# The rotation's sum of the later tiles on GpSimd, and the clamp as a paired maximum on VectorE

## The chip, the core and the metric

The kernel runs on one core of a Trainium2 chip. A core has TensorE (matrix products into PSUM), VectorE, ScalarE (activations), GpSimd and SyncE (which issues transfers), each with its own queue of instructions in the order in which the program gives them; they meet only by semaphores. All read and write SBUF; TensorE writes PSUM. The metric is the device time of one execution in microseconds (us). In the profile TensorE is PE, VectorE DVE, ScalarE ACT, GpSimd POOL.

## What is computed

Four stages on 4 x 512 tokens of 128 numbers, each `x = x + f(layernorm(x))`: a linear recurrence, a stack of two attention and feed-forward layers with a window of 64 tokens, one full attention, and a mixture of 32 experts. The change lies in the second stage, where each layer does this to its queries and keys:

```python
def l2norm(t):
    return t / jnp.clip(jnp.linalg.norm(t, axis=-1, keepdims=True), 1e-12)
...
h = shift_token(x)
qkv = h @ wqkv
q, k, v = jnp.split(qkv, 3, axis=-1)
...
q = l2norm(q) * qs
k = l2norm(k) * ksc
...
q = q * cos * scale + rotate_half(q) * sin * scale
k = k * cos / scale + rotate_half(k) * sin / scale
```

Then come scores in windows, softmax, the product with the values, and the feed-forward part with a GELU gate.

## The kernel before

**Tiling.** The second stage is cut into blocks of 512 tokens (4 batches x 2 layers = 8 blocks) and these into 4 tiles of 128 tokens, tile n of 32. A tile's queries and keys are 128 rows x 1,024 numbers (8 heads of 64, twice).

**One tile n, by the engine that does it.**
- TensorE: the product for queries and keys (L1527, L1528), then for values (L1533).
- ScalarE: the squares (L811). VectorE: `squares_sum(n)`, sums of squares over 64 (L1085), then the clamp at 1e-24 (L1088).
- GpSimd: `inverse_lengths(n)`, the power -1/2 of the 16 clamped sums (L682), called the power here.
- VectorE: `normalise(n)` (L1093), PSUM to SBUF.
- VectorE: `scale_cos(n)`, times cosine (L1102), into `rot`. GpSimd: `rotate(n)`, the two halves times sine, swapped (L690, two instructions), into `rotb`. For tiles 0 and 1 VectorE does these too.
- VectorE: its own `rotate(n)`, `rot = rot + rotb` (L1110), called the sum.
- TensorE: `heads_T(n)`, transposes of `rot` (L1542), and the scores (L1569). VectorE: maximum and subtraction (L1115, L1118). TensorE: transposes of the probabilities (L1579). ScalarE: exponentials (L837). TensorE: times the values (L1594), transposes (L1602), the output product (L1613). VectorE: `o_out(n)`, divides by the sum (L1125, L1128).

**Order.** `layer_steps()` writes out one order of steps, and every engine's program walks through it and does its own part of each item. Step i of the tile loop does, among others: transposed probabilities of tile i, squares of tile i + 3 (`ssq`), output of tile i, `heads` of tile i + 1, the sum of tile i + 2 (`rotsum`), normalise of tile i + 3 (`norm`), feed-forward `up` with its GELU and gate (L862, L1145), scores of tile i + 1, output transposes of tile i, product for queries and keys of tile i + 4, and last `rot` of tile i + 3, where L1102 and L690 stand. Steps with i mod 4 = 3 also have the transposes of the next block (L1513, L1080) and `base`, the bias added to a block's stream on GpSimd (L698, in the second layer L702 too). Steps with i mod 4 = 0 add a block's attention output and copy half of it (L1135, L1139); i mod 4 = 1 have the statistics of the feed-forward layernorm; i mod 4 = 2 a block's result (L1650, L1154).

**The end of the loop.** Steps 28 to 31 are written out by hand, with pieces of the third stage between them. At step 27's end VectorE applies the layernorm of the third stage's batch 0 (L1037, four instructions). `split` of batch 0 follows `rot` of tile 31: GpSimd forms rests of numbers cut to bf16 (L734, L737, two each), SyncE stores them and loads them again in another layout, and TensorE's `max` takes them (L1761).

Of the kernel before, what the change touches and what calls it, by code (L numbers as in the profile page):

```python
# [10 lines left out]
ALU = mybir.AluOpType  # L11
ACT = mybir.ActivationFunctionType
AX = mybir.AxisListType

P = 128
BATCH, SEQ = 4, 512
TOK = BATCH * SEQ
NT = SEQ // P
# [5 lines left out]
LAYERS, HEADS, DH, WIN = 2, 8, 64, 64  # L24
# [28 lines left out]
EW = 2 * INTER + IC * P  # L53
SKIP = 1e30
ROUNDER = 2.0 ** 23
AHEAD, WBUF = 4, 5
ROWS_AHEAD = 8

# [13 lines left out]
def build(nc, A, out):  # L72
    with ExitStack() as ctx:
        def sb(name, shape, dt=FP):
            return ctx.enter_context(nc.sbuf_tensor(name, shape, dt))

        def sem(name):
            return ctx.enter_context(nc.semaphore(name))
# [22 lines left out]
        sq = part(region_a, 2 * INNER)  # L101
# [21 lines left out]
        rot = [part(region_r, 2 * INNER) for _ in range(2)]  # L123
        rotb = [part(region_r, 2 * INNER) for _ in range(2)]
# [22 lines left out]
        stats = [sb(f"stats{i}", [P, NT, 6]) for i in range(2)]  # L147
        mv = [sb(f"mv{i}", [P, NT, 2]) for i in range(2)]
        rstd = [sb(f"rstd{i}", [P, NT]) for i in range(2)]
        ssum = sb("ssum", [P, 2 * HEADS])  # L150
        ssum_c = [sb(f"ssum_c{i}", [P, 2 * HEADS]) for i in range(2)]
        nbias = [sb(f"nbias{i}", [P, NT]) for i in range(2)]
        zero4 = sb("zero4", [P, NT])
# [96 lines left out]
        def bank(n, width=BANK, of=1):  # L250
# [3 lines left out]
        S = {n: sem(n) for n in (  # L254
            "a_in", "tab_in", "par_in", "wqkv_in", "w_in", "warm", "ones_f", "tabs", "idn", "zero_p",
            "ln_stats", "ln_mv", "ln_eps", "ln_rstd", "ln_out", "ln_neg", "ln_act", "xnT_mm", "scanned", "bc_mm", "x1",
            "yT_mm", "hT_lo", "hT_hi", "qk_mm", "v_mm", "squared", "ssq", "ssq_c", "rnormed", "normed", "rot_a",
            "rot_bb", "rotated", "v_sb", "qkT_mm", "qT_sb", "kT_sb", "s_mm", "smax", "diffed", "pT_mm", "exped", "o_mm",
            "o_rec", "o_norm", "oT_mm", "oT_sb", "wo_mm", "y_att", "hs_lo", "hs_mm", "hs_hi", "based_y", "based",
            "hnT_mm", "hnT_sb", "up_mm", "gelued", "acted", "down_mm", "y_out", "stored")}  # L260
# [180 lines left out]
        for what, n in layer_steps():  # L441
            if what == "l1":
                what, n, i = n
# [38 lines left out]
        def need(engine, semaphore, count):  # L482

            if count > 0:
                engine.wait_ge(semaphore, count)
# [148 lines left out]
        def _(pool):  # L634
            g = nc.gpsimd
# [48 lines left out]
            def rotate(n):  # L684

                pool.wait_ge(S["normed"], n + 1)
                need(pool, S["rotated"], n - 1)
                for half in range(2):
                    dst, src, tab = turned(n, half)
                    g.tensor_tensor(dst, src, tab, ALU.mult).then_inc(S["rot_bb"], 1)  # L690

            def base(k):
                l, s = divmod(k, BATCH)
# [324 lines left out]
        def _(v):  # L1018
            d = nc.vector
# [13 lines left out]
            def norm_apply(m, src, dst):  # L1033
# [5 lines left out]
                                           ALU.subtract, ALU.mult)  # L1039
                last.then_inc(S["ln_out"], 1)  # L1040

            d.memset(ones_f[:, :], 1.0).then_inc(S["ones_f"], 1)
            for p in range(2):
                d.memset(hT[p][64:P, 0:1], 0.0)
# [37 lines left out]
            def squares_sum(n):  # L1082
                v.wait_ge(S["squared"], n + 1)
                need(v, S["ssq_c"], n)
                d.tensor_reduce(ssum[:, :], sq.rearrange("p (h d) -> p h d", d=DH), AX.X, ALU.add).then_inc(S["ssq"], 1)  # L1085
                v.wait_ge(S["ssq"], n + 1)
                need(v, S["rnormed"], n - 1)
                d.tensor_scalar(ssum_c[n % 2][:, :], ssum[:, :], 1e-24, None, ALU.max).then_inc(S["ssq_c"], 1)  # L1088

            def normalise(n):  # L1090
                v.wait_ge(S["rnormed"], n + 1)
# [109 lines left out]
            def whole(dst):  # L1201

                link(d.tensor_scalar(dst, dst, ROUNDER, None, ALU.add))
                link(d.tensor_scalar(dst, dst, -ROUNDER, None, ALU.add))

# [171 lines left out]
            for what, n in layer_steps():  # L1377
# [28 lines left out]
                            d.tensor_tensor(dst, src, tab, ALU.mult).then_inc(S["rot_bb"], 1)  # L1406
                if what == "ssq":
                    squares_sum(n)
                if what == "rotsum":
                    rotate(n)  # L1410
                if what == "scores":
                    scores_out(n)
# [621 lines left out]
```

## Time and profile before

| | |
|---|---|
| median of 3 runs | 656.52 us (655.28 to 659.74) |
| the profiled execution, its own time | 653.41 us |
| its span in the profile | 651.5 us |
| PE busy | 589.5 us (90%) |
| DVE busy | 518.1 us (80%) |
| ACT busy | 363.9 us (56%) |
| POOL busy | 302.8 us (46%) |
| granted PE clock over the span | 0.987 of full |

A row of the timeline has the start, the length, the engine, the line, the operation, output and inputs with their shapes, and the number of instructions merged; in brackets the engine's idle time ahead of it and what ended it. All times count from the span's start. The chain of waits is followed back from the last instruction: at each point to what released it, or to the instruction before it on its engine.

### The profile page before, as it was taken

To read this page: it belongs to the slowest core of one execution; us is meant where nothing else is said; L and a number is where in the kernel's file an instruction comes from. 1 tells how busy PE (TensorE), PEld (TensorE's weight loads), DVE (VectorE), ACT (ScalarE), POOL (GpSimd) and SP (SyncE) were. 2 spreads that over 40 slices of the span, in tenths; PEclk is the share of its full clock that TensorE was granted. 3 is DMA by queue.
4 is the path that set the end of the run, shared out by engine and by line. 5 is a ranking of instruction groups with operands and counts; after the bars stand their busy time and mean duration, and the time that the engine had idled before them with its cause. 6 is when DMAs were issued, how large, how long until landed. Compare 5 with 4: busy or idle time off the path is not lost.

```text
span 651.5 us, 14777 instructions
## 1 busy us (share of the span) xinstructions
PE 589.5 (90%) x5571; PEld 361.4 (55%) x5571; DVE 518.1 (80%) x919; ACT 363.9 (56%) x582; POOL 302.8 (46%) x254
## 2 busy tenths in 40 slices
PE   8787987999999999999999888898899989999994
PEld 7465655766766666667667666554223324454442
DVE  5887888988799798898888975868877776577883
ACT  0243453477566575674775673422675667744882
POOL 4464464555554545555663860524020002162886
PEclk8998999999999999999999999999999999999998
DMA  8313010010110101010010126061976336216431
GB/s 264 99 26 115 18 34 10 18 34 10 24 28 17 28 17 27 17 25 20 17 26 18 35 79 132 2 146 30 225 197 188 99 98 193 95 41 131 63 47 11
DMA packets 33298, 44.04 MB, mean 68 GB/s; under 512 B 9248, under 2 KB 24652, under 8 KB 32460
## 3 DMA queue, kind: packets, MB, share of 16 engines
q1 hardware_dynamic: 26172, 40.97, 23.9%
q0 software_dynamic: 3968, 2.12, 2.4%
q8 instruction: 45, 0.74, 0.5%
q10 hardware_dynamic: 3088, 0.01, 0.3%
q14 instruction: 25, 0.20, 0.1%
HBM read 27.54 MB, written 8.41 MB: 55 GB/s over the span
## 4 chain that ended last, share of the span: by engine, by line
PE 62%; DVE 15%; ACT 6%; issue 6%; POOL 6%; DMA 2%; DVEq 0%; POOLq 0%; SPq 0%; ACTq 0%
PE ps L1594 4%; PE ps L1641 4%; PE ps L1672 4%; PE ps L1542 4%; PE ps L1579 4%; PE ps L1533 3%; PE ps L1879 3%; PE ps L1527 3%; PE ps L1650 3%; PE ps L1613 3%; PE ps L1777 3%; PE ps L1528 3%; PE ps L1569 3%; PE ps L1761 3%; ACT region_r L918 2%
## 5 line engine op out<-in xcount | busy, mean ns | idle before, releaser
L682 POOL TENSOR_TENSOR rnorm<-ssum_c,neg_half 128x16 f32<-128x16 f32 x32 | 94.7, 2960 | 101.4 <-DVE ssum_c L1088 100.0
L690 POOL TENSOR_TENSOR region_r<-region_b,region_w 128x512 f32<-128x512 f32 x60 | 77.8, 1318 | 43.3 <-DVE region_b L1093 42.8
L1317 DVE TENSOR_REDUCE mneg<-ps 128x2 f32<-128x1024 f32 x64 | 77.5, 1221 | 19.8 <-PE ps L1761 18.8
L918 ACT ACTIVATE region_r<-ps 128x1024 f32<-128x1024 f32 x64 | 63.3, 1024 | 32.3 <-PE ps L1777 32.0
L811 ACT ACTIVATE region_w<-ps 128x1024 f32<-128x1024 f32 x32 | 32.8, 1026 | 54.1 <-PE ps L1528 51.3
L1641 PE MATMUL ps<-region_w 128*114 128x512 f32 x96 | 46.0, 604 | 6.2 <-ACT region_w L828 6.1
L647 POOL TENSOR_TENSOR var_eps<-mv,eps 128x4 f32<-128x4 f32 x20 | 4.4, 221 | 95.2 <-DVE mv L1030 95.2
L787 ACT ACT_TABLE_LOAD x37 | 47.5, 1283 | 1.4 <-PEq L2026 0.7
L774 POOL DMA_INDIRECT out<-region_r x24 | 38.3, 1595 | 18.4 <-DVE region_r L1444 11.2
L1594 PEld LDWEIGHTS ps<-region_b,pts 128*64 128x64 f32 x512 | 32.2, 138 | 24.5 <-issue 24.5
L1093 DVE TENSOR_TENSOR region_b<-ps,rnorm 128x1024 f32<-128x1024 f32 x32 | 39.1, 1223 | 8.0 <-POOL rnorm L682 6.9
L837 ACT ACTIVATE pts<-ps 128x512 f32<-128x512 f32 x64 | 34.7, 595 | 18.4 <-PE ps L1579 18.4
L1115 DVE TENSOR_REDUCE smx<-ps 128x8 f32<-128x1024 f32 x32 | 38.9, 1217 | 6.2 <-PE ps L1569 6.2
L1110 DVE TENSOR_TENSOR region_r<-region_r 128x1024 f32<-128x1024 f32 x32 | 43.2, 1351 | 0.3
L1613 PEld LDWEIGHTS ps<-region_w,oT 128*128 128x128 f32 x256 | 33.6, 192 | 15.0 <-issue 12.2
L1102 DVE TENSOR_TENSOR region_r<-region_b,region_w 128x1024 f32<-128x1024 f32 x32 | 40.9, 1278 | 0.0
L1118 DVE TENSOR_TENSOR region_b<-ps,smx 128x1024 f32<-128x1024 f32 x32 | 39.2, 1225 | 1.1
L1527 PE MATMUL ps<-region_w,hT 128*128 128x512 f32 x64 | 33.9, 612 | 6.7 <-DVE region_b L1093 5.5
L1085 DVE TENSOR_REDUCE ssum<-region_w 128x16 f32<-128x1024 f32 x32 | 38.7, 1209 | 1.2 <-ACT region_w L811 1.2
L1569 PE MATMUL ps<-region_w 64*64 64x128 f32 x1024 | 34.9, 276 | 4.9 <-ACT region_w L830 4.9
L843 ACT ACTIVATE oT<-ps 128x512 f32<-128x512 f32 x32 | 18.8, 588 | 36.5 <-PE ps L1602 36.5
L1594 PE MATMUL ps<-region_b,pts 128*64 128x65 f32 x512 | 36.6, 225 | 1.7 <-ACT pts L837 1.7
(291 smaller groups left out, 1466.7 us busy)
## 6 DMA issues: line engine op xcount, KB each, us to landing
region_w<-in_wx SPq DMA_DIRECT2D x16, 768.0 KB, 4.7
region_b<-region_w SPq DMA_DIRECT2D x56, 130.0 KB, 2.3
parts_dram<-region_b SPq DMA_DIRECT2D x6, 384.0 KB, 2.6
xs_dram<-region_w SPq DMA_DIRECT2D x1, 1548.0 KB, 7.4
region_w<-in_wqkv SPq DMA_DIRECT2D x2, 768.0 KB, 9.0
pts<-xs_dram SPq DMA_DIRECT2D x24, 64.0 KB, 2.0
region_w<-parts_dram SPq DMA_DIRECT2D x3, 384.0 KB, 6.8
region_b<-parts_dram SPq DMA_DIRECT2D x3, 384.0 KB, 7.3
```

What stands on the lines that cost most here:

```text
L682: g.tensor_tensor(rnorm[:, :], ssum_c[n % 2][:, :], neg_half[:, :], ALU.pow).then_inc(S["rnormed"], 1)
L690: g.tensor_tensor(dst, src, tab, ALU.mult).then_inc(S["rot_bb"], 1)
L787: act_(warm[:, :], ones_f[:, 0:1], function).then_inc(S["warm"], 1)
L918: act_(dst, bank(l1_bank[what, b, i], of=2), ACT.Exp).then_inc(T["ex"], 1)
L1102: d.tensor_tensor(rot[n % 2].rearrange("p (z h d) -> p z h d", z=2, h=HEADS), qn[n % 2].rearrange("p (z h d) -> p z h d", z=2, h=HEADS), t ...
L1110: d.tensor_tensor(rot[n % 2], rot[n % 2], rotb[n % 2], ALU.add).then_inc(S["rotated"], 1)
L1317: d.tensor_reduce(mneg[b % 2][:, 2 * i:2 * i + 2], bank(l1_bank[what, b, i], of=2) .rearrange("p (q t) -> p q t", q=2), AX.X, ALU.max, neg ...
L1527: mm(bank(n0), lhs, wqkv[l][:, 0:INNER], start=True, stop=True)
L1569: last = mm(bank(4 + par)[w * WIN:(w + 1) * WIN, hp * P:(hp + 1) * P], qT[p][rows, hp, q0:q0 + WIN], kT[p][rows, hp, q0:q0 + P], start=Fal ...
L1594: last = mm(ps[w * WIN:(w + 1) * WIN, c0:c0 + VW], pts[n % 2][:, j, w * WIN:(w + 1) * WIN], vals[:, t, h, :], start=True, stop=True)
L1613: last = mm(bank(3)[:, t * P:(t + 1) * P], oT[n % 2][:, c, :], wo[k // BATCH][:, c, :], start=(c == 0), stop=(c == 3))
L1641: last = mm(ps[0:HW, n0 * BANK:(n0 + 1) * BANK], w1[k // BATCH][:, g, c, :], hnT, start=True, stop=True)
```

## The change

`rot = rot + rotb` of tiles 10 to 31 is done by GpSimd, right behind its two multiplications of the same tile; for tiles 0 to 9 VectorE keeps it in its old place. The constant of the clamp is written once into every second element of `ssum`, the sums of squares are written into the others, and the clamp becomes a reduction with maximum over the pairs.

```diff
+POOL_SUMS = 2 * NT + 2
...
-        ssum = sb("ssum", [P, 2 * HEADS])
+        ssum = sb("ssum", [P, 2 * HEADS, 2])
...
                 for half in range(2):
                     dst, src, tab = turned(n, half)
                     g.tensor_tensor(dst, src, tab, ALU.mult).then_inc(S["rot_bb"], 1)
+                if n >= POOL_SUMS:
+                    pool.wait_ge(S["rotated"], n)
+                    pool.wait_ge(S["rot_a"], n + 1)
+                    pool.wait_ge(S["rot_bb"], 2 * n + 2)
+                    g.tensor_tensor(rot[n % 2], rot[n % 2], rotb[n % 2], ALU.add).then_inc(S["rotated"], 1)
...
+            d.memset(ssum[:, :, 1], 1e-24)
...
-                d.tensor_reduce(ssum[:, :], sq.rearrange("p (h d) -> p h d", d=DH), AX.X, ALU.add).then_inc(S["ssq"], 1)
+                d.tensor_reduce(ssum[:, :, 0], sq.rearrange("p (h d) -> p h d", d=DH), AX.X, ALU.add).then_inc(S["ssq"], 1)
                 v.wait_ge(S["ssq"], n + 1)
                 need(v, S["rnormed"], n - 1)
-                d.tensor_scalar(ssum_c[n % 2][:, :], ssum[:, :], 1e-24, None, ALU.max).then_inc(S["ssq_c"], 1)
+                d.tensor_reduce(ssum_c[n % 2][:, :], ssum[:, :, :], AX.X, ALU.max).then_inc(S["ssq_c"], 1)
...
-                if what == "rotsum":
+                if what == "rotsum" and n < POOL_SUMS:
                     rotate(n)
```

The order of instructions is shown at two places. VectorE, end of step 18 and step 19 before the change, from the cosine product of tile 21 on (names are those of buffers; `ps` is PSUM, `region_r` holds `rot` and `rotb`, `region_b` the normalised tile):

```order
L1102 TENSOR_TENSOR region_r<-region_b,region_w 128x1024
L1085 TENSOR_REDUCE ssum<-region_w 128x16
L1088 TENSOR_SCALAR ssum_c<-ssum 128x16
L1125 RECIPROCAL orec<-ps 128x8
L1128 TENSOR_TENSOR region_r<-ps,orec 128x512
L1080 COPY hT<-ps 64x511
L1110 TENSOR_TENSOR region_r<-region_r 128x1024
L1093 TENSOR_TENSOR region_b<-ps,rnorm 128x1024
L1145 SCALAR_TENSOR_TENSOR region_b<-ps,b,region_w 114x512
```

The same place after it (the lines of the changed kernel are numbered some 7 higher):

```order
L1109 TENSOR_TENSOR region_r<-region_b,region_w 128x1024
L1092 TENSOR_REDUCE ssum<-region_w 128x16
L1095 TENSOR_REDUCE ssum_c<-ssum 128x16
L1132 RECIPROCAL orec<-ps 128x8
L1135 TENSOR_TENSOR region_r<-ps,orec 128x512
L1087 COPY hT<-ps 64x511
L1100 TENSOR_TENSOR region_b<-ps,rnorm 128x1024
L1152 SCALAR_TENSOR_TENSOR region_b<-ps,b,region_w 114x512
```

The sum is gone from between output and normalise, and the clamp is a reduction. GpSimd, from `base` of step 27 to the split of the third stage, before:

```order
L698 TENSOR_TENSOR region_r<-y,b 128x512
L702 TENSOR_TENSOR region_r<-region_r,xr 128x512
L690 TENSOR_TENSOR region_r<-region_b,region_w 128x16x32 x2
L682 TENSOR_TENSOR rnorm<-ssum_c,neg_half 128x16
L690 TENSOR_TENSOR region_r<-region_b,region_w 128x16x32 x2
L734 TENSOR_TENSOR rot_b<-rot_b,region_r 128x512 x2
L737 TENSOR_TENSOR region_r<-rot_b,region_r 128x512 x2
```

And after:

```order
L704 TENSOR_TENSOR region_r<-y,b 128x512
L708 TENSOR_TENSOR region_r<-region_r,xr 128x512
L691 TENSOR_TENSOR region_r<-region_b,region_w 128x16x32 x2
L696 TENSOR_TENSOR region_r<-region_r 128x1024
L683 TENSOR_TENSOR rnorm<-ssum_c,neg_half 128x16
L691 TENSOR_TENSOR region_r<-region_b,region_w 128x16x32 x2
L696 TENSOR_TENSOR region_r<-region_r 128x1024
L740 TENSOR_TENSOR rot_b<-rot_b,region_r 128x512 x2
L743 TENSOR_TENSOR region_r<-rot_b,region_r 128x512 x2
```

Sums of tiles 30 and 31 (L696) now stand ahead of the power of tile 31 and ahead of the split.

## Rows read from the trace of the kernel before

**Rows 1.** Page, part 4: the chain that ended last, shares of the span by engine.

```profile
PE 62%; DVE 15%; ACT 6%; issue 6%; POOL 6%; DMA 2%; DVEq 0%; POOLq 0%; SPq 0%; ACTq 0%
```

**Rows 2.** Chain in order of time (start us, us, engine and line), steps 11, 19, 23.

```profile
179.09 2.04 DVE region_r L1110
...
270.28 2.04 DVE region_r L1110
...
272.35 0.73 DVE region_b L1093
...
276.68 1.09 PE ps L1579 x8
...
315.87 2.03 DVE region_r L1110
```

**Rows 3.** Timeline, GpSimd, steps 18 and 19 (start us, us, engine, line, operation, idle before).

```profile
256.31 2.90 POOL L682 TENSOR_TENSOR rnorm<-ssum_c,neg_half 128x16 f32<-128x16 f32 x1 [5.19 <-DVE ssum_c L1088]
...
267.10 2.90 POOL L682 TENSOR_TENSOR rnorm<-ssum_c,neg_half 128x16 f32<-128x16 f32 x1 [4.06 <-DVE ssum_c L1088]
269.97 1.27 POOL L698 TENSOR_TENSOR region_r<-region_r,b 128x512 f32<-128x512 f32 x1
```

**Rows 4.** Timeline, VectorE, step 18 and the start of step 19.

```profile
256.98 1.22 DVE L1110 TENSOR_TENSOR region_r<-region_r 128x1024 f32<-128x1024 f32 x1
259.24 1.22 DVE L1093 TENSOR_TENSOR region_b<-ps,rnorm 128x1024 f32<-128x1024 f32 x1 [1.04 <-POOL rnorm L682]
...
263.33 1.23 DVE L1118 TENSOR_TENSOR region_b<-ps,smx 128x1024 f32<-128x1024 f32 x1
264.47 1.22 DVE L1102 TENSOR_TENSOR region_r<-region_b,region_w 128x1024 f32<-128x1024 f32 x1
...
266.85 0.17 DVE L1088 TENSOR_SCALAR ssum_c<-ssum 128x16 f32<-128x16 f32 x1
```

**Rows 5.** Timeline, TensorE, steps 18 and 19: L1602, L1579, L1602.

```profile
261.92 0.66 PE L1602 MATMUL ps<-ident,region_r 128*128 128x128 f32 x4
...
265.02 1.04 PE L1579 MATMUL ps<-ident,region_b 128*128 128x128 f32 x8
...
272.89 0.66 PE L1602 MATMUL ps<-ident,region_r 128*128 128x128 f32 x4
```

**Rows 6.** Timeline, GpSimd, end of the loop (steps 27 to 29) and block 1's split.

```profile
365.66 3.48 POOL L690 TENSOR_TENSOR region_r<-region_b,region_w 128x512 f32<-128x512 f32 x2
371.41 2.91 POOL L682 TENSOR_TENSOR rnorm<-ssum_c,neg_half 128x16 f32<-128x16 f32 x1 [2.27 <-DVE ssum_c L1088]
...
378.17 3.20 POOL L734 TENSOR_TENSOR rot_b<-rot_b,region_r 128x512 f32<-128x512 f32 x2
381.34 3.25 POOL L737 TENSOR_TENSOR region_r<-rot_b,region_r 128x512 bf16<-128x512 f32 x2
...
420.79 2.31 POOL L734 TENSOR_TENSOR pts<-pts,region_b 128x512 f32<-128x512 f32 x2 [4.31 <-ACT region_b L899]
```

**Rows 7.** Timeline, VectorE, end of the loop.

```profile
366.75 1.27 DVE L1102 TENSOR_TENSOR region_r<-region_b,region_w 128x1024 f32<-128x1024 f32 x1
367.94 2.06 DVE L1037 TENSOR_SCALAR y<-xr,mv,rstd 128x128 f32<-128x128 f32 x4
...
377.89 1.35 DVE L1102 TENSOR_TENSOR region_r<-region_b,region_w 128x1024 f32<-128x1024 f32 x1
```

**Rows 8.** Timeline, TensorE, the first scores of the next layer.

```profile
399.73 0.59 PE L1761 MATMUL ps<-region_w 96*128 96x512 bf16 x2 [0.47 <-DMA region_w<-parts_dram]
```

**Rows 9.** Timeline ahead of step 0: tile 2's products on GpSimd, then VectorE beside them.

```profile
42.00 4.39 POOL L690 TENSOR_TENSOR region_r<-region_b,region_w 128x512 f32<-128x512 f32 x2 [2.07 <-DVE region_b L1093]
...
41.84 1.22 DVE L1110 TENSOR_TENSOR region_r<-region_r 128x1024 f32<-128x1024 f32 x1
42.97 2.29 DVE L1102 TENSOR_TENSOR region_r<-region_b,region_w 128x1024 f32<-128x1024 f32 x1
45.18 1.21 DVE L1085 TENSOR_REDUCE ssum<-region_w 128x16 f32<-128x1024 f32 x1
```

## The prediction, made before the changed kernel was run

> **What bounds the kernel now.** I read the chain of waits first, by engine. It stands on TensorE for 62% of the span and on VectorE for 15% [rows 1], so VectorE work is worth time only where it is on that 15%.
>
> The chain in order of time shows where that is. A step is one pass of the tile loop. In the step that ends a block's four tiles, the chain leaves TensorE and runs through the rotation's sum (L1110), normalise, gated product, maximum and subtraction on VectorE before TensorE goes on with L1579, the first work of the next step [rows 2]. The sum takes 2.03 to 2.04 us there, and 1.22 elsewhere [rows 4]; so it is in four steps, 11, 15, 19 and 23, of which rows 2 show the first and the last. The reason is beside it: GpSimd's L698 starts at 269.97 for 1.27 us [rows 3], and the sum issued at 270.28 ends at 272.32, about 1.1 us after L698. The two engines do not read side by side. In the other three steps of four the chain stays on TensorE: the subtraction started at 263.33 ends at 264.56, and TensorE takes it up at 265.02 [rows 4, 5], 0.46 us to spare.
>
> **What the change removes.** The sums of tiles 10 to 31 leave VectorE: 22 instructions. Where TensorE leads nothing is gained. In step 19 normalise of tile 22 no longer stands behind the sum (start 272.35, rows 2) but behind the power alone. How much TensorE can use of that: from L1602 to L1579 it takes 265.02 - 261.92 = 3.10 us unhindered, and 276.68 - 272.89 = 3.79 out of step 19 [rows 2, 5]. So the gain is at most 0.69 us a step, 4 × 0.69 = 2.8 us. It is reached if the subtraction ends 0.7 us earlier. Normalise will start 1.2 us earlier (next part); the gated product then waits for its GELU, but the maximum can still start about 1.0 us earlier, so TensorE is the limit and I take all 2.8.
>
> **What it adds on GpSimd, in a usual step.** The trace has no 128x1024 add on GpSimd. The nearest rows: an add of 128x512 takes 1.27 us, so 2.5 for the double [rows 3]; the plain 128x512 pieces at 420.79 take 2.31 for two [rows 6], the lower bound; the upper is the 4.39 us of two products where VectorE holds the reads twice [rows 9]. I take 2.5, since what follows L1102 on VectorE, a reduction and small work, has one input in SBUF. Sum(21) waits for L1102, which ends at 264.47 + 1.22 = 265.69; with 0.08 us for the signal it runs 265.77 to 268.27. Power(22), queued behind it, starts now at 267.10 when the clamp is done [rows 3, 4]; it will start at 268.25: 1.15 us late. Who waits is normalise. In step 18 it starts when the power ends (259.24, after 1.04 us idle, rows 4), so it comes at 260.4 and ends at 261.6; a small output add follows, and the maximum slips 0.1 us, within the 0.46 to spare. That leaves the sum some 0.35 us: the cost is 0 while it stays under about 2.85 us, and I take 0. In steps 20 and 21 VectorE idles about 1 us before the gated product, for its GELU, and that takes the delay. In step 19 the power ends at 271.15 and normalise starts there, 1.2 us earlier than now, as used above. TensorE transposes tile n a whole step later, so that the sum itself comes later costs nothing.
>
> A page of the Trainium skill prices it a little lower: GPSIMD Engine Reference, § 3.1, has an add of 2,048 columns at 4,497 ns, so an estimate of 2.25 us for 1,024. No run here shows it; the loss below would shrink by some 0.5 us.
>
> **The clamp.** A reduction over pairs replaces the 0.17 us scalar maximum [rows 4]: 16 more numbers read. A reduction of 1,024 columns takes 1.21 us [rows 9], so some 0.02 us more, 0.6 us over 32 tiles, in the idle time named; were it 0.2 more each, it would still be inside 0.35. It runs while the new sum reads. The reduction at 45.18 ran its 1.21 us beside a product that ended at 46.39 [rows 9], so I let it pass undelayed. A scalar form would wait: L1037's four took 2.06 us, started behind GpSimd's products [rows 6, 7]. The one memset, before any input has landed, costs nothing.
>
> **What it adds at the end of the loop.** Here GpSimd leads. The products of tile 30 end at 369.14; power(31) starts at 371.41; the split of the next layer (L734, L737) begins at 378.17 behind the products of tile 31 and ends at 384.59; its store and load end in TensorE's L1761 at 399.73, after only 0.47 us of idle [rows 6, 8]. So all delay of this chain above 0.47 us arrives. Two sums enter it.
> - Power(30) is 1.15 late as before, so L702 ends at 366.8. VectorE's L1102 (issued 366.75, rows 7) reads next, then a product, one L1037, a product, one L1037, sum(30), two L1037. That alternation is what rows 9 show: at 43.0 GpSimd's waiting product went between two back-to-back VectorE instructions, and the second of these (2.29 us) went before the next product. Then L1037 ends at about 373.85 and not 370.00, and power(31), behind L1085 and the clamp, starts at 375.3: 3.9 late. If VectorE keeps its turn for all four L1037, sum(30) runs 371.5 to 374.0, and power(31) is 2.6 late.
> - Sum(31) waits for L1102 of tile 31, now 377.89 to 379.24 [rows 7], which is pushed with normalise(31) to end at 383.1 (or 381.8). The sum ends at 385.6 (384.3), and the split's four pieces, with L1110 of tile 31 gone from VectorE, take 4 × 1.15 = 4.6 and not 6.4 us [rows 6]. They end at 390.2 (388.9), 5.6 (4.3) later than 384.59.
> - TensorE itself is some 2 to 4 us late by then, so not all of this is idle time; 0.1 is lost in what cover is left. Loss 5.5, or 4.2.
>
> **Sum.** -2.8 + 5.5 = +2.7 us, or -2.8 + 4.2 = +1.4. I take +2.5, near the first, since rows 9 show the alternation. The profiled execution took 653.41 us (span 651.5), so it would become 655.9; the runs shown have the median 656.52, so 659.0.
>
> **Rivals.**
> - *The end loses nothing (faster, small).* Were the store and load to absorb the delay, only the gain is left: 656.5 - 2.8 = 653.7. For it: the landing of a transfer varies with what else is queued. Against: 0.47 us of idle before L1761 is all the cover there is.
> - *The power becomes late for TensorE in every step (slower).* If the sum takes 3.5 us, it is 0.65 above what the cover allows, in some 14 steps that gain nothing: 9 us; the gain falls by 1 and the end costs 2 more: 656.5 + 2.5 + 12 = 671. It decides from 2.85 us on. For it: the 4.39 us at 42.00. Against: nothing with two SBUF inputs stands behind L1102 on VectorE except at step 27.
> - *The power holds the reads.* At the end of the loop the copy L1139 will fall into power(31). Did it wait for the power's end, normalise(31) would come behind copy, reciprocal and a 512-column product, about 1.1 us: 659.0 + 1.1 = 660.1. Against: the sum issued at 256.98 took 1.22 us while the power ran from 256.31 to 259.21 [rows 3, 4], so I add nothing. The Trainium skill (SBUF — State Buffer, § Who interferes with whom) says that whoever issues first gets the shared pair "for the whole instruction"; on the power the trace disagrees.
> - *More gain than TensorE's room.* If the shorter VectorE queue drew in other waits, 0.3 us in each of 22 tiles, it would be 659.0 - 6.6 = 652.4. Against: those waits are not on the chain.
>
> **Numbers.** Forecast (+1.4 to +2.7) 0.60; end loses nothing 0.18; power holds the reads 0.06; power late in every step 0.07; more gain 0.09. One per cent, 6.5 us, is what a measurement of this kernel can tell from no change. The slow rival (0.07) lies outside it, and so may 0.05 on the fast side: the tail of the last kind, or the gain alone with a low draw of runs, which themselves span 655.3 to 659.7. So faster 0.05, same 0.88, slower 0.07. The range takes in the gain alone and the held reads, with that spread: 653.0 to 662.5. The likeliest case's own range is 656 to 661.
>
> **What would show it.** In the changed profile: sums of 2.5 us on GpSimd; TensorE's L1579 behind steps 11, 15, 19 and 23 not waiting for VectorE, so a four-tile period of 44.9 us, not the 45.6 from 270.28 to 315.87; the other steps as long as now; power starts 1.1 us late; the L1037 group at step 27 stretched to 4 to 6 us; the split ending 4 to 6 us later against the end of step 26, and TensorE idle before the first L1761 for 1.5 to 3 us. It is wrong if the sum is longer than 2.85 us, if the load lands no later, or if TensorE's steps shorten elsewhere.

## The result, and the profile after

| | before | after |
|---|---|---|
| median, measured side by side | 659.34 us (9 runs, 655.28 to 661.79) | 665.47 us (9 runs, 662.36 to 666.32) |
| ratio | | 1.011, interval 1.0085 to 1.0138 |
| span of the profiled execution | 651.5 us | 663.7 us |
| VectorE busy | 518.1 us | 496.4 us |
| GpSimd busy | 302.8 us | 351.3 us |
| granted clock over the span | 0.987 | 0.975 |

The change makes the kernel 6 us slower, outside the range of the prediction (653.0 to 662.5). The kernel after, put on the chip a second time beside others, gave 664.62 us against 657.08 for before, a ratio of 1.014 (1.0105 to 1.0175).

The rows of cost first, from the groups of the page of the kernel after (busy us and mean ns, then the idle time ahead and what ended it). The lines moved by seven or so: the sum on GpSimd is L696, the power L683, normalise L1100, the cosine product L1109, the clamp L1095.

```profile
L683 POOL TENSOR_TENSOR rnorm<-ssum_c,neg_half 128x16 f32<-128x16 f32 x32 | 95.2, 2976 | 21.1 <-DVE ssum_c L1095 19.7
...
L696 POOL TENSOR_TENSOR region_r<-region_r 128x1024 f32<-128x1024 f32 x22 | 52.1, 2367 | 44.4 <-DVE region_r L1109 44.3
L1100 DVE TENSOR_TENSOR region_b<-ps,rnorm 128x1024 f32<-128x1024 f32 x32 | 39.2, 1224 | 44.2 <-POOL rnorm L683 44.0
```

A sum takes 2.37 us on GpSimd, against 1.22 us on VectorE where nothing is in its way [rows 4]. VectorE now idles 44 us for the power.

**The steady part of the loop came out as forecast.** The same place as [rows 3 to 5], steps 18 and 19, in the timeline of the kernel after: GpSimd, then VectorE, then TensorE.

```profile
267.24 2.36 POOL L696 TENSOR_TENSOR region_r<-region_r 128x1024 f32<-128x1024 f32 x1 [1.73 <-DVE region_r L1109]
269.55 2.91 POOL L683 TENSOR_TENSOR rnorm<-ssum_c,neg_half 128x16 f32<-128x16 f32 x1
...
267.03 1.21 DVE L1092 TENSOR_REDUCE ssum<-region_w 128x16 f32<-128x1024 f32 x1
268.27 0.18 DVE L1095 TENSOR_REDUCE ssum_c<-ssum 128x16 f32<-128x32 f32 x1
...
272.50 1.23 DVE L1100 TENSOR_TENSOR region_b<-ps,rnorm 128x1024 f32<-128x1024 f32 x1 [0.82 <-POOL rnorm L683]
...
274.32 0.66 PE L1609 MATMUL ps<-ident,region_r 128*128 128x128 f32 x4
...
277.42 1.04 PE L1586 MATMUL ps<-ident,region_b 128*128 128x128 f32 x8
```

The power starts 1.1 us behind the end of the clamp (269.55 against 268.45), the reduction and the clamp run beside the sum at their usual 1.21 and 0.18 us, and in step 19 TensorE's L1586 follows the product ahead of it with no wait: 277.42 - 274.32 = 3.10 us where it took 3.79 before [rows 5]. From the scores of tile 8 to those of tile 27 the trace has 213.91 us after and 216.79 before: 2.88 us gained, forecast 2.8.

**The end of the loop lost 8.5 us, not 5.5.** By chance both traces have the scores of tile 28 at 363.10 us. The first scores of the third stage (L1761 before, L1768 after) start at 399.73 before [rows 8] and at 408.19 after. The change of the loop thus makes -2.9 + 8.5 = 5.6 us, where the two measurements have 6.1 and 7.5. The spans of the two traces differ by 12.2 us, since 2.9 us more lie ahead of the scores of tile 8 after, and 3.7 us more behind the first scores of the third stage. None of the moved sums stands there, and the paired clamp, which does stand in the first part, isn't the cause: the kernel only_30, below, has it too and reaches the scores of tile 8 at 133.74 us, before does at 135.34.

TensorE after, in the timeline from the scores of tile 28 on:

```profile
363.10 1.04 PE L1576 MATMUL ps<-region_w 64*64 64x128 f32 x32
...
375.00 1.22 PE L1631 MATMUL ps<-region_r,down_one 128*128 128x256 f32 x2 [3.81 <-DVE region_r L1142]
...
378.80 1.92 PE L1576 MATMUL ps<-region_w 64*64 64x128 f32 x32
...
390.91 1.42 PE L1576 MATMUL ps<-region_w 64*64 64x128 f32 x32 [2.77 <-ACT region_w L836]
...
393.17 4.50 PE L1648 MATMUL ps<-region_w 128*114 128x512 f32 x8
...
408.19 0.60 PE L1768 MATMUL ps<-region_w 96*128 96x512 bf16 x2
```

The same place before:

```profile
371.98 0.70 PE L1624 MATMUL ps<-region_r,down_one 128*128 128x256 f32 x2 [0.80 <-DVE region_r L1135]
...
374.30 1.04 PE L1569 MATMUL ps<-region_w 64*64 64x128 f32 x32
...
383.33 1.10 PE L1569 MATMUL ps<-region_w 64*64 64x128 f32 x32 [0.85 <-ACT region_w L830]
...
384.85 3.60 PE L1641 MATMUL ps<-region_w 128*114 128x512 f32 x8
```

Three things are to be seen. TensorE idles 3.81 us (before 0.80) ahead of the token shift of the attention output, and 2.77 us (before 0.85) ahead of the scores of tile 30. The same instructions take longer behind each idle time: 1.92 us for the scores that took 1.04, 4.50 for the feed-forward product that took 3.60. And L1768 waits for nothing: the transfer, on which the prediction hung the loss, has landed when TensorE comes. It landed late all the same. The loads, as SyncE issued them after:

```profile
L579 SPq DMA_DIRECT2D region_w<-parts_dram x6: 335/421/423, 395.6 to 397.9; - x6
...
DMA to landing us min/median/max: 4.6/7.8/9.4
```

The last of them was issued at 397.9 and took 9.4 us to land, so it was there at 407.3, 0.9 us ahead of L1768. Before, the last was issued at 390.1 and was there at 399.6. So this path is 7.7 us later too, and TensorE's own is only a little later still.

The window view gives the granted clock (the column ahead of the last two, DMA share and GB/s) of the stretch 353 to 400 us, before and then after, and of 375 to 380 us after:

```profile
core 0: us, PE busy (x) PEld busy (x) DVE busy (x) ACT busy (x) POOL busy (x), PEclk, DMA share, GB/s
353.00:400.00 47.00, 41.43 (x462) 29.99 (x455) 37.03 (x61) 27.87 (x45) 24.77 (x20) 1.00 0.34 74
```

```profile
353.00:400.00 47.00, 38.13 (x352) 26.09 (x344) 32.32 (x54) 24.65 (x40) 30.90 (x23) 0.89 0.18 43
...
375.00:380.00 5.00, 4.53 (x36) 3.32 (x40) 2.30 (x4) 1.16 (x2) 3.66 (x3) 0.50 0.01 3
```

Behind the idle time of 3.81 us TensorE ran at 0.50 of full, the lower of its two levels, 1.2 GHz in place of 2.4. Why it idled stands in the timeline of GpSimd, VectorE and ScalarE after, at the same place as [rows 6, 7]:

```profile
370.28 2.38 POOL L696 TENSOR_TENSOR region_r<-region_r 128x1024 f32<-128x1024 f32 x1 [0.17 <-POOL region_r L691]
374.43 2.91 POOL L683 TENSOR_TENSOR rnorm<-ssum_c,neg_half 128x16 f32<-128x16 f32 x1 [1.77 <-DVE ssum_c L1095]
...
384.55 2.36 POOL L696 TENSOR_TENSOR region_r<-region_r 128x1024 f32<-128x1024 f32 x1 [3.38 <-DVE region_r L1109]
386.87 2.27 POOL L740 TENSOR_TENSOR rot_b<-rot_b,region_r 128x512 f32<-128x512 f32 x2
389.09 2.27 POOL L743 TENSOR_TENSOR region_r<-rot_b,region_r 128x512 bf16<-128x512 f32 x2
...
366.75 2.23 DVE L1109 TENSOR_TENSOR region_r<-region_b,region_w 128x1024 f32<-128x1024 f32 x1
368.90 4.10 DVE L1043 TENSOR_SCALAR y<-xr,mv,rstd 128x128 f32<-128x128 f32 x4
...
374.27 0.68 DVE L1142 TENSOR_TENSOR region_r<-region_r,ps 128x512 f32<-128x512 f32 x1
...
388.06 0.63 ACT L911 ACTIVATE region_r<-rot_b 128x512 bf16<-128x512 f32 x1 [2.15 <-POOL rot_b L740]
...
389.70 0.58 ACT L834 ACTIVATE region_w<-ps 128x512 f32<-128x512 f32 x1
```

The third stage's four multiply-subtracts (L1043) take 4.10 us and not 2.06 [rows 7]. The longest of them took 1.29 us before, beside GpSimd's second product. After, one took 2.37 us, from 370.38 on, beside the sum of tile 30, which ends at 372.66. L1142, the addition of a block's attention output, is queued behind all four on VectorE, and TensorE's L1631 waits for it. One step on, ScalarE's two copies of the heads of tile 30 (L834, L836) are queued behind its two casts (L911), which wait for GpSimd's split, which stands behind sum(31); TensorE's scores of tile 30 wait for the copies.

### The profile page after: what moved, and what is told of

It is laid out like the page before. It is cut to its first block, busy times and chain, and to the rows that moved or that the text cites. A ratio compares the mean times of both kernels' runs of the same rounds, so it can differ in the third digit from the quotient of the medians.

```text
span 663.7 us, 14778 instructions
## 1 busy us (share of the span) xinstructions
PE 594.2 (90%) x5571; PEld 365.4 (55%) x5571; DVE 496.4 (75%) x898; ACT 364.0 (55%) x582; POOL 351.3 (53%) x276
## 4 chain that ended last, share of the span: by engine, by line
PE 67%; DVE 13%; ACT 7%; issue 6%; POOL 5%; DMA 1%; POOLq 0%; DVEq 0%; SPq 0%; ACTq 0%
PE ps L1648 6%; PE ps L1601 4%; PE ps L1679 4%; PE ps L1549 4%; PE ps L1576 4%; PE ps L1620 3%; PE ps L1534 3%; PE ps L1657 3%; PE ps L1586 3%; PE ps L1535 3%; PE ps L1540 3%; PE ps L1886 3%; PE ps L1784 3%; PE ps L1768 3%; PE ps L1609 3%
## 5 line engine op out<-in xcount | busy, mean ns | idle before, releaser
L683 POOL TENSOR_TENSOR rnorm<-ssum_c,neg_half 128x16 f32<-128x16 f32 x32 | 95.2, 2976 | 21.1 <-DVE ssum_c L1095 19.7
L696 POOL TENSOR_TENSOR region_r<-region_r 128x1024 f32<-128x1024 f32 x22 | 52.1, 2367 | 44.4 <-DVE region_r L1109 44.3
L1100 DVE TENSOR_TENSOR region_b<-ps,rnorm 128x1024 f32<-128x1024 f32 x32 | 39.2, 1224 | 44.2 <-POOL rnorm L683 44.0
L1648 PE MATMUL ps<-region_w 128*114 128x512 f32 x96 | 46.9, 614 | 6.2 <-ACT region_w L834 6.1
L1576 PE MATMUL ps<-region_w 64*64 64x128 f32 x1024 | 36.8, 285 | 6.3 <-ACT region_w L836 6.3
L1109 DVE TENSOR_TENSOR region_r<-region_b,region_w 128x1024 f32<-128x1024 f32 x32 | 42.0, 1311 | 0.0
```

The costliest lines, as they stand in the source:

```text
L683: g.tensor_tensor(rnorm[:, :], ssum_c[n % 2][:, :], neg_half[:, :], ALU.pow).then_inc(S["rnormed"], 1)
L696: g.tensor_tensor(rot[n % 2], rot[n % 2], rotb[n % 2], ALU.add).then_inc(S["rotated"], 1)
L1109: d.tensor_tensor(rot[n % 2].rearrange("p (z h d) -> p z h d", z=2, h=HEADS), qn[n % 2].rearrange("p (z h d) -> p z h d", z=2, h=HEADS), t ...
L1576: last = mm(bank(4 + par)[w * WIN:(w + 1) * WIN, hp * P:(hp + 1) * P], qT[p][rows, hp, q0:q0 + WIN], kT[p][rows, hp, q0:q0 + P], start=Fal ...
L1648: last = mm(ps[0:HW, n0 * BANK:(n0 + 1) * BANK], w1[k // BATCH][:, g, c, :], hnT, start=True, stop=True)
```

## The experiments

A stretch is taken from each trace here: "front" from the start of the scores of tile 8 to those of tile 27, "end" from the scores of tile 28 to the first scores of the third stage. Outside these two places the granted clock of a single execution dips at other places too, so single spans are not compared. The changed kernel's condition `n >= POOL_SUMS` became a set of tiles. In every such kernel VectorE's own sums also wait for the sum of the tile before, since that one may be GpSimd's.

| kernel | sums on GpSimd | front, us | end, us | ratio to before (interval) |
|---|---|---|---|---|
| before | none | 216.79 | 36.63 | 1 |
| clamp_alone | none | 216.86 | 36.76 | 0.999 (0.996 to 1.002) |
| after | 10 to 31 | 213.91 | 45.09 | 1.011 (1.0085 to 1.014) |
| last_two_only | 30, 31 | 216.84 | 44.35 | 1.013 (1.009 to 1.017) |
| only_30 | 30 | 216.83 | 39.82 | 1.0045 (1.001 to 1.008) |
| only_31 | 31 | 216.82 | 41.20 | 1.010 (1.007 to 1.013) |
| heads_first_31 | 31 | 216.87 | 37.66 | 1.005 (1.0015 to 1.008) |
| after_kept_busy | 10 to 31 | 213.91 | 41.44 | 1.010 (1.007 to 1.013) |
| keep_last_two | 10 to 29 | 213.91 | 38.92 | 1.000 (0.997 to 1.0025) |
| keep_last_three | 10 to 28 | 213.90 | 36.27 | 0.999 (0.997 to 1.002) |
| scalar_clamp | 10 to 28 | 214.69 | 37.16 | 1.002 (0.999 to 1.005) |
| from_9 | 9 to 28 | 213.37 | 36.68 | 0.996 (0.993 to 0.999) |

### The end of the loop undone: keep_last_two

```diff
-POOL_SUMS = 2 * NT + 2
+POOL_SUMS = range(2 * NT + 2, NTILES - 2)
...
-                if n >= POOL_SUMS:
+                if n in POOL_SUMS:
...
             def rotate(n):
+                need(v, S["rotated"], n)
                 v.wait_ge(S["rot_a"], n + 1)
...
-                if what == "rotsum" and n < POOL_SUMS:
+                if what == "rotsum" and n not in POOL_SUMS:
```

> VectorE keeps the sums of tiles 30 and 31, GpSimd has those of tiles 10 to 29. Theory A (the loss is made at the end of the loop by the two last sums alone; the four steps that end a block gain 0.7 us each): 2.8 us faster than the kernel before, ratio 0.996, no TensorE wait above 1 us between the end of step 27 and the first scores of the next layer beyond those of before. Theory B (sums on GpSimd cost in every step, or the paired clamp does): slower than before by 1 us or more.

Measured: 657.74 us, ratio 1.000, so theory A had the main part and missed the time: it put the whole loss on the two last sums. The gain of the front is whole and 6.2 of the 8.5 us of the end are gone. 2.3 us stay, of which 1.6 lie between the scores of tiles 28 and 29 (12.80 us against 11.20). TensorE there, in its timeline:

```profile
374.79 0.70 PE L1632 MATMUL ps<-region_r,down_one 128*128 128x256 f32 x2 [1.75 <-DVE region_r L1143]
...
377.76 1.87 PE L1577 MATMUL ps<-region_w 64*64 64x128 f32 x32
```

The idle time is 1.75 us (0.80 before), and the scores take 1.87 us for 1.04. Sum(29), ahead of power(30) in GpSimd's queue, does that: in keep_last_three, below, it is VectorE's again and the 2.3 us are gone.

### The last two sums alone: last_two_only

```diff
-POOL_SUMS = 2 * NT + 2
+POOL_SUMS = range(NTILES - 2, NTILES)
```

> Only the sums of tiles 30 and 31 are on GpSimd, tiles 0 to 29 are VectorE's as before; the paired clamp stays. Theory A: the whole loss of the end and no gain: 8 to 10 us slower than before (ratio 1.013 to 1.015), slower than the changed kernel by about 2.8 us. Theory B: less than 3 us slower, since 20 of the 22 sums are back.

Measured: 667.85 us, ratio 1.013; end 44.35 us, so 7.7 us lost by two instructions, and nothing gained at the front. Its median is 2.4 us above that of the changed kernel, which has nearly the same loss and the gain, though the intervals overlap. Theory A forecast this.

### The clamp alone: clamp_alone

```diff
-POOL_SUMS = 2 * NT + 2
+POOL_SUMS = range(0)
```

> All sums on VectorE as before, only the clamp as maximum over pairs (and the memset). Theory A: no change, ratio 0.999 to 1.001. If the clamp is the cause of a part of the loss, or shifts the first 130 us, where the changed kernel's profile was 2.9 us behind: 1 to 3 us slower.

Measured: 657.94 us, ratio 0.999 (0.996 to 1.002), front and end within 0.13 us of before. The clamp over pairs takes 186 ns on average and the scalar one took 175: 0.4 us over 32 tiles, hidden.

### The clock: after_kept_busy, twice

```diff
+                if (what, n) == ("scores", NTILES - 2):
+                    keep_busy_b(2, 12)
                 if what == "scores":
                     scores(n)
...
+                if (what, n) == ("shift", BLOCKS - 2):
+                    keep_busy_b(2, 16)
                 if what == "shift":
                     shifted(n)
```

This is the changed kernel with filler matmuls of 128x512 in TensorE's two idle times, 16 in the first (ahead of the token shift) and 12 in the second (ahead of the scores of tile 30). Their results are read by nobody.

> The changed kernel, and TensorE multiplies an identity (16 and 12 products that nobody reads) in the two places where it stood idle for 3.8 and 2.8 us at the end of the loop. Theory C (the idle time lets the granted clock fall to half, and that is a large part of the loss there): the granted clock stays at 1.0 from 370 to 400 us, and the kernel is 2.5 to 4 us faster than the changed one (ratio to before about 1.006). Theory D (only the waits themselves cost, the clock is a bystander): as slow as the changed kernel, ratio 1.011.

TensorE's timeline of this kernel:

```profile
369.44 3.62 PE L1492 MATMUL ps<-ident_b 128*128 128x512 bf16 x16
373.42 0.70 PE L1631 MATMUL ps<-region_r,down_one 128*128 128x256 f32 x2 [0.37 <-DVE region_r L1142]
...
375.75 1.04 PE L1576 MATMUL ps<-region_w 64*64 64x128 f32 x32
...
383.85 2.76 PE L1492 MATMUL ps<-ident_b 128*128 128x512 bf16 x12
387.18 1.10 PE L1576 MATMUL ps<-region_w 64*64 64x128 f32 x32 [0.57 <-ACT region_w L836]
...
388.71 3.60 PE L1648 MATMUL ps<-region_w 128*114 128x512 f32 x8
```

Measured: 664.39 us in four runs. The scores are back at 1.04 and 1.10 us, L1648 at 3.60, the clock of 353 to 400 us at 1.00, and the end is 41.44 us. So of the 8.5 us, 3.65 were the clock's and 4.8 the plain waits': 3.0 between the scores of tiles 28 and 29, 2.4 between those of 29 and 30, and 0.6 back ahead of L1768. But the time was hardly lower than the 665.47 us without filler, so both kernels went on the chip again, side by side:

> The changed kernel once more, unaltered, beside its kept-busy form on one chip. From the traces so far: 2.9 us gained by the scores of tile 27, 8.5 us lost from the scores of tile 28 to the first scores of the last stage, so 5.6 us over before, ratio 1.0085. If TensorE's clock at the end of the loop is settled by its idle times there, the trace shows again 1.8 to 2.0 us for the scores of tile 29 and a stretch of 44.5 to 45.5 us.

> The changed kernel with filler matmuls in its two idle times at the end of the loop, in more rounds, since its four timed runs before gave 664.4 us where its trace would have given 661. Theory (the clock's fall costs 3.6 of the 8.5 us): the stretch is again 41.4 us, and the time is 3 to 4 us under that of the unaltered kernel on the same chip, ratio to before 1.003 to 1.005. Rival (the clock's fall is only put off to a later place, so that it costs as much elsewhere): the trace shows 41.4 us for the stretch, and the times stay within 1.5 us of the unaltered kernel's, ratio 1.007 to 1.01.

Measured: 664.62 us for the changed kernel (1.014, interval 1.0105 to 1.0175) and 663.36 us with the filler (1.010, interval 1.006 to 1.013). The ends are 45.13 and 41.48 us: the stretch repeats to 0.05 us. The time of the changed kernel is again further above before than the 1.0085 that its traces give. The medians differ by 1.3 us, within the 1.5 us of the rival, but the two intervals overlap, and the ratios lie 0.004 apart, which is 2.8 us. So these times don't decide between the theory's 3.65 us and the rival. From the first scores of the third stage to the end of the span the two traces of the changed kernel have 255.5 and 254.9 us, those with the filler 257.5 and 257.3, which is 2.2 us more on average. But over all fourteen traces this rest of the execution goes from 251.8 us (before) to 258.2 (last_two_only), and clamp_alone has 255.9 with an end like that of before, so two traces each don't show that the filler makes the 2.2 us. The window view of one place in it, in the second traces of the changed kernel and of the one with filler:

```profile
598.00:622.00 24.00, 22.43 (x232) 11.08 (x232) 17.75 (x40) 15.32 (x36) 10.79 (x8) 1.00 0.56 113
```

```profile
598.00:622.00 24.00, 21.49 (x225) 10.47 (x223) 15.43 (x35) 14.97 (x35) 8.61 (x7) 0.93 0.53 100
```

Some 200 us later the clock dips in both executions of the kernel with filler and in neither of the changed kernel. It isn't the filler's alone: clamp_alone and last_two_only have 0.93 there as well. What decides it stays open, and so does whether the filler only moves the clock's fall to a later place.

### One of the two sums each: only_30 and only_31

```diff
-POOL_SUMS = 2 * NT + 2
+POOL_SUMS = range(30, 31)
```

> GpSimd makes one sum of the rotation only, that of tile 30, with the paired clamp; all others are VectorE's. last_two_only lost 7.7 us between the scores of tile 28 and the first scores of the last stage (44.35 against 36.63 before). Theory (the first of the two sums holds up what stands behind it: VectorE's four multiply-subtracts of the normalised rows take 4.10 us in place of 2.06, TensorE then waits 3.8 us for the attention output of tile 27, and its clock falls): this kernel shows most of the loss, 4 to 6 us of the 7.7, so a stretch of 41 to 43 us and a ratio of 1.006 to 1.009. Rival (what costs is the sum of tile 31, which stands ahead of the split and so of ScalarE's casts and copies): the stretch stays below 38.5 us and the ratio below 1.003.

Measured: 661.24 us, ratio 1.0045; end 39.82 us, 3.2 lost, between the two forecasts. My theory that this sum makes most of the loss fell: it makes less than half. Its mechanism held: VectorE's four take 4.10 us, and TensorE waits 2.86 us.

```profile
366.38 4.10 DVE L1043 TENSOR_SCALAR y<-xr,mv,rstd 128x128 f32<-128x128 f32 x4
...
372.48 0.70 PE L1632 MATMUL ps<-region_r,down_one 128*128 128x256 f32 x2 [2.86 <-DVE region_r L1143]
```

The idle time of this one wait adds up: 0.80 us before; 1.75 with sum(29), so 0.95 for it; 2.86 with sum(30), so 2.06 for it; and 3.81 after, which is 0.80 + 0.95 + 2.06.

The other one has `range(31, 32)`:

> GpSimd makes the sum of tile 31 only, with the paired clamp. Theory: the sum stands ahead of the split on GpSimd and puts it off by 1 to 3.5 us; ScalarE's casts, its copies of the heads behind them and the scores of tile 31 follow, so the stretch from the scores of tile 28 to the first scores of the last stage is 38 to 40 us against 36.63, ratio 1.002 to 1.005. Together with the kernel that has only the sum of tile 30 it should make up the 7.7 us of last_two_only, or less if the clock's fall is shared. Rival: this sum makes the greater part, 41 us or more.

Measured: 663.77 us, ratio 1.010; end 41.20 us, 4.6 lost, so the rival was right. 3.2 + 4.6 = 7.8 against the 7.7 of last_two_only. GpSimd, ScalarE and TensorE in its timeline:

```profile
380.07 2.35 POOL L696 TENSOR_TENSOR region_r<-region_r 128x1024 f32<-128x1024 f32 x1 [1.22 <-DVE region_r L1109]
382.38 2.27 POOL L740 TENSOR_TENSOR rot_b<-rot_b,region_r 128x512 f32<-128x512 f32 x2
...
383.57 0.63 ACT L911 ACTIVATE region_r<-rot_b 128x512 bf16<-128x512 f32 x1 [2.65 <-POOL rot_b L740]
...
386.42 1.99 PE L1577 MATMUL ps<-region_w 64*64 64x128 f32 x32 [3.26 <-ACT region_w L836]
...
389.25 5.23 PE L1649 MATMUL ps<-region_w 128*114 128x512 f32 x8
```

The scores of tile 30 are 2.4 us late, and another 2.8 us are lost up to those of tile 31, by a feed-forward product that takes 5.23 us for 3.60 and scores that take 1.99 for 1.10. At the end 0.6 come back.

### The same late split, past ScalarE: heads_first_31

```diff
-                29: [("probs", 29), ("ff_stats", 6), *l1("split"), ("vals", 29), ("heads", 30), ("rotsum", 31), ("ff_rstd", 6),
+                29: [("probs", 29), ("ff_stats", 6), ("vals", 29), ("heads", 30), *l1("split"), ("rotsum", 31), ("ff_rstd", 6),
```

> As only_31 (GpSimd makes the sum of tile 31 alone), but in the program's order the split stands behind the heads of tile 30, so that ScalarE makes the two copies of the heads before its two casts, which wait for GpSimd's split; GpSimd's own order is the same, sum(31) ahead of the split. Theory (the loss of 4.6 us in only_31 came through ScalarE: casts 2.65 us idle, copies of the heads 2.4 us late, TensorE 3.26 us idle and its clock at half): the scores of tile 30 come at the distance of before (9.0 us behind those of tile 29), TensorE keeps its clock, and what remains is the split's end, 2 to 3 us late, with the store and the load behind it: the stretch is 37 to 39.5 us with a DMA wait ahead of the first scores of the last stage, ratio 1.001 to 1.004. Rival (GpSimd's late split or the rotation's sum reaches TensorE by another way): 40.5 us or more.

Measured: 659.25 us, ratio 1.005 (1.0015 to 1.008), against only_31's 663.77 on the same change to the sums. ScalarE and TensorE in its timeline:

```profile
382.49 0.60 ACT L834 ACTIVATE region_w<-ps 128x512 f32<-128x512 f32 x1 [1.87 <-PE ps L1550]
...
383.46 0.63 ACT L911 ACTIVATE region_r<-rot_b 128x512 bf16<-128x512 f32 x1
...
383.72 1.10 PE L1577 MATMUL ps<-region_w 64*64 64x128 f32 x32 [0.86 <-ACT region_w L836]
...
401.13 0.59 PE L1769 MATMUL ps<-region_w 96*128 96x512 bf16 x2 [1.47 <-DMA region_w<-parts_dram]
```

With the copies ahead of the casts the scores of tile 30 come 9.03 us behind those of tile 29, as before; the clock of 353 to 400 us stays at 1.00; and only 1.0 us is lost, at the first scores of the third stage, which now do wait 1.47 us for the transfer (0.47 before). That is the mechanism of the prediction, seen alone for this one sum, and it is the small part of the 4.6 us that only_31 lost. The new order was not run without the sum, nor with both sums, so what the transfer alone would cost beside sum(30) and sum(31) together isn't shown.

### Which sums pay: keep_last_three and from_9

```diff
-POOL_SUMS = 2 * NT + 2
+POOL_SUMS = range(2 * NT + 2, NTILES - 3)
```

> GpSimd makes the sums of tiles 10 to 28, VectorE those of 29, 30 and 31. keep_last_two still lost 2.3 us from the scores of tile 28 on, and there GpSimd's power of tile 30 began at 374.22 us behind a chain that the sum of tile 29 stood in. Theory (that sum is the cause): the stretch from the scores of tile 28 to the first scores of the last stage is back at 36.6 to 37.2 us, the 2.9 us gained by tile 27 stay, and the time is 2.5 to 2.9 us under the one of before: ratio 0.9955 to 0.997. Rival (the paired clamp or something else at the end costs it): the stretch stays at 38.9 us and the ratio at 0.9995 to 1.0.

Measured: 656.83 us, where before gave 657.92 (31 runs); ratio 0.999 (0.997 to 1.002). The trace is a little better than the theory had it: front 213.90, end 36.27, together 3.25 us under before. The times show 1.1 us with an uncertainty of 1.7, so they neither show the gain nor exclude most of it.

from_9 has `range(9, NTILES - 3)`:

> GpSimd makes the sums of tiles 9 to 28, with the paired clamp: keep_last_three with one tile more at the front, where the step from the scores of tile 8 to those of tile 9 takes 11.51 us and not 10.97. Theory: that step too comes to about 11.0 us, so the trace shows 3.4 us gained by tile 27 and nothing lost behind it, 3.4 to 3.8 us under before, ratio 0.9945 to 0.997. Rival (at step 7 TensorE is late for another reason, the feed-forward's shift not being filled): 11.51 us stays, and the kernel equals keep_last_three, ratio 0.996 to 1.0.

Measured: 654.60 us where before gave 657.08 (25 runs); ratio 0.996 (0.993 to 0.999). The step from the scores of tile 8 to those of tile 9 takes 10.98 us and not 11.51, so the front is 213.37 us, 3.4 under before. The end is 36.68, as before, with 0.46 us of DMA wait ahead of the first scores of the third stage. This is the one kernel here whose interval lies below 1: 2.5 us faster than before, with 0.7 to 4.3 us as the interval.

### The scalar clamp beside GpSimd's sum: scalar_clamp

The sums on GpSimd as in keep_last_three, and

```diff
-                d.tensor_reduce(ssum_c[n % 2][:, :], ssum[:, :, :], AX.X, ALU.max).then_inc(S["ssq_c"], 1)
+                d.tensor_scalar(ssum_c[n % 2][:, :], ssum[:, :, 0], 1e-24, None, ALU.max).then_inc(S["ssq_c"], 1)
```

> As keep_last_three, but the clamp is the scalar maximum of the kernel before, so that the one change between the two is the form of the clamp while GpSimd adds. Theory (the prediction's: the paired form is there because the scalar one would have to wait for GpSimd's sum): the clamp of tiles 10 to 28 ends with GpSimd's sum, some 0.5 to 1.2 us later than the paired one, GpSimd's power starts later still, and the step of 10.97 us grows by up to 1.2 us where it has no slack left: 0 to 15 us in all; I take 5 us over keep_last_three. Rival (the two forms take the same beside GpSimd): no difference, within 0.5 us in the traces.

The clamp in VectorE's timeline at the end of step 18, first of this kernel, then of keep_last_three:

```profile
266.07 1.36 DVE L1095 TENSOR_SCALAR ssum_c<-ssum 128x16 f32<-128x16 f32 x1
```

```profile
269.13 0.19 DVE L1095 TENSOR_REDUCE ssum_c<-ssum 128x16 f32<-128x32 f32 x1
```

The scalar maximum takes 1.36 us and ends at 267.43, GpSimd's sum at 267.40; the paired one takes 0.19. So it does wait. What this costs is less than the 5 us that I took. The front grows by 0.8 us: 0.6 from the scores of tile 24 to those of 25 (11.60 us for 10.97) and 0.2 from those of tile 8 to those of 9. It isn't more, since the power is queued behind the sum on GpSimd in either form and can hardly start sooner. The end grows by 0.9 us, all of it in a wait of 0.91 us for the load ahead of the first scores of the third stage; whether the clamp's form makes that, one trace doesn't show. The times are 659.33 and 656.83 us with overlapping intervals; no more than the two stretches can be told.

## Why the prediction was wrong, step by step

- **Gain at steps 11, 15, 19 and 23, 2.8 us.** Right: 2.88, with L1586 not waiting and a four-tile period of 307.24 - 262.38 = 44.86 us (forecast 44.9).
- **Usual steps cost nothing, sum of 2.5 us, power 1.15 late.** Right: 2.37 us, 1.1 late. The Trainium skill's figure (GPSIMD Engine Reference, § 3.1), from which an estimate of 2.25 us was made, lies 0.12 below the measured one; the plain rows had given 2.5, 0.13 above.
- **The clamp.** Right, by clamp_alone; and scalar_clamp shows that the scalar form would have waited.
- **The power holds the reads.** It does not: the copy L1146 at 374.98 us took 0.29 us while the power ran from 374.43 to 377.34, as the trace before had said, against the rule of the Trainium skill (SBUF — State Buffer, § Who interferes with whom).
- **GpSimd's chain at the end.** The order was right. The sum did go between VectorE's four (4.10 us; I had them end 3.85 us late, they ended 3.0 late), and power(31) began 3.0 us late, between the two forecasts of 3.9 and 2.6. The split ended at 391.36 and not 384.59 us, 6.8 late where 5.6 was forecast: VectorE's maximum of tile 29 had to wait 2.2 us for scores that TensorE made late and slowly, and all behind it went with it.
- **Where the loss arrives.** This is the main step that failed: "all delay of this chain above 0.47 us arrives", by the store and load ahead of the first scores of the third stage, and "TensorE itself is some 2 to 4 us late by then, so not all of this is idle time; 0.1 is lost in what cover is left". I took one arrival, the last, and let TensorE's own lateness only cover it. The transfer did come late, even later than forecast: 7.7 us (407.3 against 399.6). But TensorE was not 2 to 4 us late by then: it came at 408.19, where before it would have been ready at 399.26 (399.73 less its 0.47 us of idle), so 8.9 us late, and it was the last to arrive. In fact the delay reached TensorE at two earlier places, where what it waits for is queued behind delayed work on a third engine: the attention output behind L1043 on VectorE (3.0 us, of which 0.95 are sum(29)'s), and the copies of the heads behind the casts on ScalarE (2.4 us). ScalarE does not stand in the sum at all, though it has the casts of that same split. TensorE never waited for the transfer; in heads_first_31, with one of the sums and the way through ScalarE closed, it did, for 1.0 us more than before.
- **The clock.** This is the second step that failed. The granted clock fell behind each of the two idle times, and that made 4.8 us into 8.5 within the stretch (after_kept_busy). The sum had no term for it, although every us of new idle time on TensorE at that place was a reason to ask. In the medians only 1.3 us of those 3.65 were seen when the clock was kept up, with overlapping intervals; whether the rest came back elsewhere stays open.
- **The level.** The forecast stood on a median of three runs, 656.52; beside the changed kernel before gave 659.34, so the forecast's +2.5 would have been 661.8, within the range. 2.8 of the 6.5 us between forecast and result are thus the draw of runs for the kernel before. The remaining 3.6 us are the term above, 8.5 for 5.5, and 0.6 that the traces do not place. That the forecast's loss of 5.5 lies near the 4.8 of the plain waits is luck, since it was put on another path.

Of the rivals none had this. "The power holds the reads" (660.1) and "the power becomes late for TensorE in every step" (671) were the nearest in time, 5.4 and 5.5 us off, by mechanisms that did not occur.

## What to carry to other kernels

When an instruction is added to a queue, list what is queued behind the *waiting* work on every other engine, and not just the one chain that seems to end last: two of 22 moved additions (tiles 30 and 31) cost 7.7 us here, mostly through VectorE's and ScalarE's queues, while the other twenty gained 2.9 at the front, and one of them (tile 29) cost 2.6 at the end. Moving work in a steady loop and at its end are two changes, and a condition on the tile separates them at no cost that was seen. When several paths run into one instruction, work out the lateness of each, and not only of the one that ended last before. And when new idle time on TensorE is forecast, ask what the work behind it costs at the lower clock: here 0.95 us of it made 1.6 from the scores of tile 28 to those of tile 29. The traces show that within the stretch; for the time of the whole kernel the runs don't settle it.

## What the runs showed of the hardware

- **TensorE's clock.** An idle time of 0.80 us left the scores behind it at 1.04 us. Idle times of 1.75, 2.86 and 3.81 us at the same place were followed by scores of 1.87, 1.77 and 1.92 us. With the idle time filled by 3.62 us of matmuls, 0.37 us of it left, they took 1.04. At the second place, ahead of the scores of tile 30, it did not always show in the scores themselves: behind 3.26 us (only_31) they took 1.99, behind 2.77 (after) 1.42, and behind 2.49 (after_again) 1.10 as before, with 4.99 for 3.60 us in the feed-forward product that follows.
- **One VectorE instruction can wait out a GpSimd addition between two of its kind.** Of the four L1043 of the third stage, which took 2.06 us together before, the shortest took 0.33 and the longest 2.37 us, as long as the sum beside it. Four of the same form with no GpSimd instruction beside them, at 254.08 us of the kernel after, took 1.10 us together.
- **Which forms wait.** Beside a GpSimd addition, VectorE's reductions ran at 1.21 and 0.18 us, a scalar maximum of 16 numbers took 1.36 us in place of 0.17, and the copy L1146 at 280.19 us took 0.67 us (0.29 beside the power), ending 0.15 us behind the sum that ran from 278.34 to 280.71.
